# Attention of eight heads: divide the exponentials before they are transposed, with a new order of the whole pipeline

## The reference

```
hid = _group_norm(xr, norm_w, norm_b)
qkv = jnp.einsum('oc,bcl->bol', qkv_w, hid) + qkv_b[None, :, None]
qkv = qkv.reshape(b, H, 3, ch, L)
q, k, v = (qkv[:, :, 0], qkv[:, :, 1], qkv[:, :, 2])
weight = jnp.einsum('bhct,bhcs->bhts', q * scale, k * scale)
weight = jax.nn.softmax(weight.astype(jnp.float32), axis=-1)
a = jnp.einsum('bhts,bhcs->bhct', weight, v)
h = jnp.einsum('oc,bcl->bol', proj_w, a.reshape(b, c, L)) + proj_b[None, :, None]
return (x + h) / RESCALE
```

## Time and profile before

| | |
|---|---|
| median of 3 runs | 2169.7 us (2168.6 to 2170.22) |
| the profiled execution | 2170.37 us, of which span 2168.3 us |
| mean granted TensorE clock | 0.976 |
| busy: PE, DVE, ACT, POOL | 2076.3, 1820.4, 1527.8, 1278.3 us |
| share of the ending chain by engine | PE 91%, DVE 3%, POOL 2% |

### The profile page before, as it was taken

One profiled execution on the slowest core, in us unless ns is written; L12 is line 12 of the kernel. 1 busy time (PEld: TensorE's weight loads), 2 busy tenths in 40 slices (PEclk: granted clock), 3 DMA queues, 4 the chain that ended last, 5 costly groups with the idle time before them and its releaser, 6 DMA issues.

```text
span 2168.3 us, 58678 instructions
## 1 busy us (share of the span) xinstructions
PE 2076.3 (96%) x15232; PEld 1686.7 (78%) x15232; DVE 1820.4 (84%) x4359; ACT 1527.8 (70%) x5172; POOL 1278.3 (59%) x2954
## 2 busy tenths in 40 slices
PE   4679999999999999999999999999999999999987
PEld 3466888888888788888878888887888888788775
DVE  6778899988888998988899898888989888887532
ACT  2256777777777777777777777777777777777763
POOL 2455666666666666666666666666666666664311
PEclk8799999999999999999999999999999999999977
DMA  3000011001101100110110011011101100100000
GB/s 126 15 23 23 16 39 39 29 23 37 37 22 37 37 30 22 37 37 22 37 37 30 22 37 37 23 36 37 37 15 37 37 31 28 38 31 24 24 23 23
DMA packets 29828, 70.22 MB, mean 32 GB/s; under 512 B 6261, under 2 KB 7105, under 8 KB 29761
## 3 DMA queue, kind: packets, MB, share of 16 engines
q1 hardware_dynamic: 26928, 67.68, 9.0%
q10 hardware_dynamic: 2832, 1.73, 0.3%
HBM read 30.86 MB, written 12.85 MB: 20 GB/s over the span
## 4 chain that ended last, share of the span: by engine, by line
PE 91%; DVE 3%; POOL 2%; issue 2%; ACT 1%; SPq 1%; DMA 0%; POOLq 0%; DVEq 0%; ACTq 0%
PE ps_c L1166 19%; PE ps_a L1166 17%; PE ps_e L1166 17%; PE ps_b L1166 17%; PE ps_s L1166 10%; PE ps_s L1216 8%; POOL gn_t L579 1%; PE ps_a L1292 1%; DVE y L1158 1%; PE ps_e L1454 0%; PE ps_e L1292 0%; PE ps_b L1454 0%; PE ps_e L1399 0%; SPq L475 0%; ACT e L827 0%
## 5 line engine op out<-in xcount | busy, mean ns | idle before, releaser
L827 ACT ACTIVATE e<-ps_s,nm 98x196 f32<-98x196 f32 x1024 | 426.1, 446 | 89.9 <-DVE nm L956 89.8
L590 POOL TENSOR_SCALAR xn<-x,gn_scale,gn_shift 128x196 f32<-128x196 f32 x384 | 353.2, 933 | 20.8 <-POOL gn_shift L585 20.8
L1158 DVE SCALAR_TENSOR_TENSOR y<-opad,w_dw,y 128x406 f32<-128x406 f32 x512 | 301.8, 645 | 0.0
L1139 DVE SCALAR_TENSOR_TENSOR y<-xpad,w_dw,y 128x406 f32<-128x406 f32 x512 | 300.8, 640 | 0.0
L956 DVE TENSOR_REDUCE nm<-ps_s 98x4 f32<-98x784 f32 x256 | 240.6, 962 | 41.8 <-PE ps_s L1166 41.8
L834 ACT COPY pt<-ps_s 98x392 f32<-98x392 f32 x512 | 229.1, 503 | 42.6 <-PE ps_s L1216 41.8
L568 POOL TENSOR_TENSOR gn_t<-gn_group 128x4 f32<-128x4 f32 x96 | 34.3, 358 | 372.9 <-DVE gn_group L1006 286.5
L827 ACT ACTIVATION_READ_ACCUMULATOR e<-ps_s,nm 98x1 f32 x1024 | 231.6, 226 | 0.0
L1216 PE MATMUL ps_s<-w_eye,e 98*98 98x98 f32 x2048 | 204.6, 251 | 0.6 <-ACT e L827 0.6
L1216 PEld LDWEIGHTS ps_s<-w_eye,e 98*98 98x98 f32 x2048 | 186.3, 131 | 24.1 <-issue 16.2
L581 POOL TENSOR_SCALAR gn_t<-gn_t 128x4 f32<-128x4 f32 x288 | 119.7, 416 | 58.6 <-POOL gn_t L579 58.6
(11 more groups left out here) (245 smaller groups left out, 5596.8 us busy)
## 6 DMA issues: line engine op xcount, KB each, us to landing
x_in<-in_x SPq DMA_DIRECT2D x32, 392.0 KB, 3.1
x_res<-in_x SPq DMA_DIRECT2D x32, 392.0 KB, 3.3
x2b<-x SPq DMA_DIRECT2D x32, 392.0 KB, 2.6
out<-x SPq DMA_DIRECT2D x32, 392.0 KB, 2.6
out_pairs<-out SPq DMA_DIRECT2D x32, 392.0 KB, 3.5
w_q<-in_q SPq DMA_DIRECT2D x3, 256.0 KB
w_k<-in_k SPq DMA_DIRECT2D x3, 256.0 KB
w_v<-in_v SPq DMA_DIRECT2D x3, 256.0 KB
```

The lines of the kernel that those rows point to most:

```text
L590: g.tensor_scalar(dst[:, c, of_image(i)], src[:, c, of_image(i)], t.scale[:, j:j + 1], t.shift[:, j:j + 1], ALU.mult, ALU.add).then_inc(t. ...
L827: s.activation(e2[:, j, tc], tile(use)[0:HALF, of_image(tc)], ACT.Exp, bias=nm2[:, j, tc:tc + 1], accum_out=den2[:, 2 * i + tc, h:h + 1]). ...
L1139: v.scalar_tensor_tensor(out=dst, in0=window(xpad, c, k, CR), scalar=tap, in1=dst, op0=ALU.mult, op1=ALU.add).then_inc(conv1_steps.sem, 1)
L1158: v.scalar_tensor_tensor(out=dst, in0=window(opad, c, k, CR), scalar=tap, in1=dst, op0=ALU.mult, op1=ALU.add).then_inc(conv2_steps.sem, 1)
```

## The change

The exponentials of a head are divided by their sums in place, in `e2`, before PE transposes them. For this DVE takes reciprocals eight times a pair, for two heads each (`rden{g}_{m}`); heads 0 and 2 of each pass are then scaled by ACT (`less{g}_0`, `less{g}_2`), heads 1 and 3 by POOL (`less{g}_1`, `less{g}_3`), two instructions of 98x196 a head. The transposes wait for the scaled tiles. The steps `rden`, `rt`, `rep0`, `rep1`, their buffers and the weight `heads` go, and `proj` reads `a2`. All five tables have new numbers, and the shared PSUM banks a, b, c, e have new uses; the largest place is 819 instead of 760, so a pair now spans one table step more.

```diff
+                    for four in range(GROUPS):
+                        for j in range(1, HG, 2):
+                            p = pair_of(t, u, POOL_AT[f"less{four}_{j}"])
+                            if p is not None:
+                                h = HG * (four % 2) + j
+                                pool.wait_ge(rden_done.sem, rden_done.at(p, 2 * four + j // 2 + 1))
+                                for tc in range(2):
+                                    alone()
+                                    g.tensor_scalar(e2[:, j, tc], e2[:, j, tc], rden2[:, 2 * (four // 2) + tc, h:h + 1], None,
+                                                    ALU.mult).then_inc(p2_done[j].sem, 1)
...
-                    p = pair_of(t, u, ACT_AT["rt"])
-                    if p is not None:
-                        act.wait_ge(*full(p, "rt"))
-                        if has_before(p) and not comes_after("rt", latest("rep0", "rep1")):
-                            act.wait_ge(*full(p - 1, latest("rep0", "rep1")))
-                        s.copy(rt2[:, 0], tile("rt")[0:H2, 0:N2]).then_inc(rt_high.sem, 1)
...
+                            p = pair_of(t, u, ACT_AT[f"less{g}_{j}"]) if j % 2 == 0 else None
+                            if p is not None:
+                                h = HG * (g % 2) + j
+                                act.wait_ge(rden_done.sem, rden_done.at(p, 2 * g + j // 2 + 1))
+                                for tc in range(2):
+                                    s.activation(e2[:, j, tc], e2[:, j, tc], ACT.Copy,
+                                                 scale=rden2[:, 2 * i + tc, h:h + 1]).then_inc(p2_done[j].sem, 1)
...
+                            p = pair_of(t, u, DVE_AT[f"rden{g}_{m}"])
+                            if p is not None:
+                                for j in (2 * m, 2 * m + 1):
+                                    dve.wait_ge(*read(p, f"sc{g}_{j}"))
+                                h = HG * (g % 2) + 2 * m
+                                v.reciprocal(rden2[:, 2 * i:2 * i + 2, h:h + 2], den2[:, 2 * i:2 * i + 2, h:h + 2]
+                                             ).then_inc(rden_done.sem, 1)
...
-                                for source in elsewhere(use, f"sc{g}_{j}"):
-                                    pe.wait_ge(*read(p, source))
+                                pe.wait_ge(p2_done[j].sem, p2_done[j].at(p, 2 * g + 2))
...
-                            product(tile(use)[:, 0:N2], lambda k: heads[:, c], lambda k: rt2[:, k]).then_inc(filled(use), 1)
...
-                            product(tile(use)[:, 0:N2], lambda k: w["p2"][:, k, of_chunk(c)], lambda k: an2[:, :, k]
+                            product(tile(use)[:, 0:N2], lambda k: w["p2"][:, k, of_chunk(c)], lambda k: a2[:, :, k]
```

More of the change, by code:

```diff
@@ L104 @@
     "qb2": (128, KC), "kb2": (128, KC), "vb2": (128, KC), "p2": (128, KC, CH), "pb2": (128, KC),
-    "heads": (H2, KC, 128), "eye": (128, 128),
+    "eye": (128, 128),
     "gn3_w": (128, 4), "gn3_b": (128, 4), "q3": (128, KC, CH), "k3": (128, KC, CH), "v3": (128, KC, CH),
@@ L358, in build @@
         max2_done = Count("max2_done", UNITS // 2)
-        rden_done = Count("rden_done", 1)
-        rt_high = Count("rt_high", 1)
+        rden_done = Count("rden_done", 2 * GROUPS)
+        p2_done = [Count(f"p2_done{j}", 2 * GROUPS) for j in range(HG)]
         l3_less_steps = Count("l3_less_steps", 2 * 3)
@@ L660, in split_weights @@
                     s.copy(high, src).then_inc(early_high, 1)
-                s.copy(heads[:], w["heads"][:]).then_inc(early_steps, 1)
                 act.wait_ge(early_steps, EARLY_STEPS)
@@ L839, in step @@
                             if has_before(p):
-                                act.wait_ge(*read(p - 1, f"rep{g % 2}"))
+                                act.wait_ge(*full(p - 1, latest("proj0", "proj1")))
                             s.copy(a2[:, i, g % 2], tile(use)[:, 0:TOK]).then_inc(emptied(use), 1)
@@ L1051, in step @@
                                                    in1=xn1[:, c], op0=ALU.add, op1=ALU.add).then_inc(emptied(use), 1)
-                    p = pair_of(t, u, DVE_AT["rden"])
-                    if p is not None:
-                        for use in ends(*(f"sc{g}_{j}" for g in range(GROUPS) for j in range(HG))):
-                            dve.wait_ge(*read(p, use))
-                        if has_before(p):
-                            dve.wait_ge(*full(p - 1, "rt"))
-                        v.reciprocal(rden2[:], den2[:]).then_inc(rden_done.sem, 1)
-                    p = pair_of(t, u, DVE_AT["rt"])
-                    if p is not None:
-                        dve.wait_ge(rt_high.sem, rt_high.at(p, 1))
-                        v.tensor_tensor(rt2[:, 1], tile("rt")[0:H2, 0:N2], rt2[:, 0], ALU.subtract).then_inc(emptied("rt"), 1)
-                    for c in range(KC):
-                        use = f"rep{c}"
-                        p = pair_of(t, u, DVE_AT[use])
-                        if p is not None:
-                            dve.wait_ge(*full(p, use))
-                            if has_before(p) and not comes_after(use, latest("proj0", "proj1")):
-                                dve.wait_ge(*full(p - 1, latest("proj0", "proj1")))
-                            for source in ends(f"av{c}", f"av{2 + c}"):
-                                dve.wait_ge(*read(p, source))
-                            v.tensor_tensor(an2[:, :, c], tile(use)[:, 0:N2].rearrange("p (i n) -> p i n", i=2),
-                                            a2[:, :, c], ALU.mult).then_inc(emptied(use), 1)
+                    for g in range(GROUPS):
+                        i = g // 2
+                        for m in range(2):
+                            p = pair_of(t, u, DVE_AT[f"rden{g}_{m}"])
[5 more added lines that the diff above has]
+                                             ).then_inc(rden_done.sem, 1)
                     for c in range(KC):
@@ L1392, in step @@
                                ).then_inc(filled(use), 1)
-                    p = pair_of(t, u, PE_AT["rt"])
-                    if p is not None:
-                        pe.wait_ge(*free(p, "rt"))
-                        pe.wait_ge(rden_done.sem, rden_done.at(p, 1))
-                        for j in range(4):
-                            last = nc.tensor.transpose(tile("rt")[0:H2, j * HALF:(j + 1) * HALF], rden2[:, j],
-                                                       eye[0:HALF, 0:HALF])
-                        last.then_inc(filled("rt"), 1)
-                    for c in range(KC):
-                        use = f"rep{c}"
-                        p = pair_of(t, u, PE_AT[use])
-                        if p is not None:
-                            pe.wait_ge(*free(p, use))
-                            for source in elsewhere(use, "rt"):
-                                pe.wait_ge(*read(p, source))
-                            product(tile(use)[:, 0:N2], lambda k: heads[:, c], lambda k: rt2[:, k]).then_inc(filled(use), 1)
                     for c in range(KC):
@@ L1414, in step @@
                             pe.wait_ge(*free(p, use))
[L1415 removed]
+                            for source in elsewhere(use, *(f"av{g}" for g in range(GROUPS))):
                                 pe.wait_ge(*read(p, source))
[L1417 removed]
+                            product(tile(use)[:, 0:N2], lambda k: w["p2"][:, k, of_chunk(c)], lambda k: a2[:, :, k]
                                     ).then_inc(filled(use), 1)
```

19 lines of the change are left out of this document (7 added, 12 removed), and 73 rows, old and new, of tables (ACT_AT, BANK_USES, DVE_AT, PE_AT).

## The result

| | before | after |
|---|---|---|
| median | 2169.76 us (4 runs) | 2241.84 us (2240.12 to 2243.65, 4 runs) |
| ratio | | 1.0333 (95%: 1.032 to 1.0346) |
| span of the profiled execution | 2168.3 us | 2238.0 us |
| mean granted TensorE clock | 0.976 | 0.974 |

The change makes the kernel 3.3% slower. Forecast were 2178 us with a range to 2208, so the side was the more probable one, but the size is 72 us against 8.

A forecast was written before the change was run, and what follows sets the result against it. PE, never waiting, was taken as the bound with a period of 63.08 us. 63.08 - 1.17 + 1.3 + 0.1 = 63.31, and 31 x 0.23 = 7 us over the profiled execution gave 2178 us, range 2138 to 2208.

The forecast's parts named there:

- the side: Whole run: slower was given chance 0.46, faster 0.38, within 0.2% of no change 0.16.
- PE's period of before, PE as the bound: Loop before the change: PE never waits, its sequence is the 63.08 us period; no other engine becomes the bound by sum.
- gn1's chain, the hold by the taps, the queue behind it: Pass 0: DVE's taps hold POOL's xn, four done at 11.4 us; POOL's scalings and ACT's thirteen instructions follow late.
- 16 instructions ... 0.49 from start to start: POOL's added scalings, priced like xn at 0.49 us each, 7.9 us a pair; one operation less maybe cheaper.
- All else on PE stays, reordered: PE: only the reciprocals' transposes and spreading products leave, 1.17 us a pair, 36 us if nothing takes it back.
- Rival 3: Removed PE work leaves, but an unseen place takes about its size back or more, or another engine's order decides; chance 0.07.
- The stall, 1.3 + 0.1 us: PE waiting each pair: 1.3 us in pass 0 (bounds 0 to 3.4), 0.1 in passes 1 to 3 (0 to 0.4).
- Rival 1: POOL passes between DVE's taps, so pass 0 stalls only 0 to 0.8 us: 2146 us, range 2134 to 2160; chance 0.34.
- Rival 2: POOL is held in more passes, pass 2 too, costing 1.5 to 3 us a pair on top: 2239 us; chance 0.15.
- Filling and draining I cost at nothing: Start and end of the run: no added time, as DVE's first tap to last output is 762 places instead of 759.
- 31 periods are 1955 of 2170 us: Whole run before: 31 full periods, the rest filling and draining, so a change of the period counts 31 times.

The follow-up runs named there:

- experiment 3: Changed kernel, POOL scaling head 1 of each pass with two operations in place, head 3 with one operation into its own tensor: 2236.68 us.
- experiment 6: Changed kernel with both of POOL's heads scaled in place by two operations (times the reciprocal, plus 0.0): 2233.35 us, ratio 1.029.
- experiment 2: Kernel before, old order, with the division left out (no reciprocals, turning, spreading or multiplication): 2142.61 us, ratio 0.9871.
- experiment 1: Changed kernel, new order, with all 32 scalings of a pair left out, the eight reciprocals kept: 2194.63 us, ratio 1.0108.
- experiment 9: Kernel of experiment 6 with three steps moved: DVE's second reciprocals of pass 0 and ACT's head 2 scaling earlier, an L3 scaling later: 2227.51 us, ratio 1.0268.
- experiment 4: Changed kernel with heads 1 and 3 of pass 0 scaled by ACT as well, POOL keeping six heads: 2235.94 us, ratio 1.0302.
- experiment 8: Kernel of experiment 1 with two of PE's steps that waited for a shared bank put later: 2199.21 us, ratio 1.0138.

## Why the prediction was wrong

- **PE's period of before, PE as the bound; the side.** Right. With idle PE the period grew, and the excess stands where forecast first.
- **gn1's chain, the hold by the taps, the queue behind it.** The times are right to 0.3 us in three places (8.5, 10.5, 11.4), and so was the place of the stall: heads 1 and 3 of pass 0. The hold itself was mild: the four `xn1` take 2.90 us, of which the first starts beside the last of the eight taps, and none is held over a run of them. Of the lateness 0.9 us are the taps' by this (2.90 against four times 0.5), the rest is the chain's.
- **"16 instructions ... 0.49 from start to start", lower bound 0.4.** This term failed: 0.77 to 0.80. The rows offered xn, 128x196 with two operations, as the nearest, and I let the missing operation count as a saving. It costs 0.35 us (experiment 3). The bound should have been open upward, too. It made PE's wait for POOL 1.47 us a period instead of 0.2, but for the time that is 8 us (experiment 6): the price was wrong, and a right one would not have saved the forecast.
- **"All else on PE stays, reordered": 1.17 us a pair gained.** This is the step that failed most. It treats PE's sequence as a sum of durations that an order does not alter. The removed work is worth 0.78 in the old order (experiment 2), and the new order costs 1.20 of its own before a single scaling is in it (experiment 1). Pass 0 alone is 15.01 us long without scalings, not 14.3. Rival 3 named this case, "takes about its size back or more", and gave it 0.07.
- **The stall, 1.3 + 0.1 us.** The scalings cost 1.53 together, all in pass 0, inside the bounds given. That the size fits is luck in part: the argument had POOL's instruction at 0.49 us. With one of 0.43 (experiment 6) pass 0 loses 0.6 us and not 1.3, and pass 1 loses 0.5 more, which the argument did not foresee. The idle time was forecast as the price of one late engine; in truth three links stand within a microsecond of each other (POOL's scaling, ACT's queue, DVE's reading of proj0), so that taking POOL's away gives 8 us and ACT's 6 more (experiments 6, 9).
- **Rival 1** did not come: all of POOL's work in pass 0 was done as late as forecast, no earlier. **Rival 2** did not come either in its form: PE's waits for POOL are two a period, both in pass 0. That its 2239 us lie 3 from the measured time is chance.
- **"Filling and draining I cost at nothing."** The draining became 2.1 us shorter. The filling took 19.9 us more, the second term that was put at nothing and was not. The argument compared places of DVE's table from the first tap to the last output, and these say nothing of how long the engines wait in the filling. What holds them there I could not show.
- **"31 periods are 1955 of 2170 us."** Not so: there are 27 periods of 63.1 us, and the 31 intervals together are 1900.5. A change of the period counts 27 times in full, not 31.
- The sum, then, by experiments 1 and 2: the removed work gave 28 us instead of 36, the new order took 52 instead of nothing, the scalings 47 instead of 1.4 x 31 = 43. The forecast's 7 us and these 8 + 52 + 4 make 71, and 72 were measured. The last term comes close though it counts 31 periods: 1.53 x 27 is 41 of the 47 us, 2.4 stand in the filling (271.2 against 268.8), most of the rest in the draining.

## What to carry to other kernels

Split a change that comes with a new order before pricing it: run the old order without the removed work, and the new order without the added work. The difference between these two is the order's own price, which the sum of durations did not give here; it was 52 us, more than the 28 that the removed work gave. Then compare the two kernels stretch by stretch from start to start, since the waits with names were only 0.06 us a period apart. In this kernel, with four engines busy for 79 to 97% and every bank shared, removing 1.3 us of waits gave back 0.16 us a period (experiment 6), 1.5 us gave 0.17 (experiment 4), 0.5 us gave 0.25 (experiment 9), and 0.4 us gave nothing (experiment 8): ask for the next two links before counting a gain. And bound an instruction form that the trace does not show upward as well, even where it does less.

## What was unexpected of the hardware

GpSimd's multiplication of 98x196 fp32 by a per-partition factor took 0.77 to 0.78 us as one operation and 0.43 as two (with + 0.0), in one program, on the same data type (experiment 3). ScalarE's scaling of the same tile took 0.36 from start to start, as in L3. And a small instruction of gn1's chain on GpSimd, where the ten behind it in that chain take 0.20 to 0.51 us, started at 927.98 beside a maximum and was done at 929.89. GpSimd, then DVE, in the changed kernel:

```profile
927.98 1.91 POOL L580 TENSOR_TENSOR gn_t<-gn_y 128x4 f32<-128x4 f32 x1
```

```profile
926.65 1.20 DVE L1137 SCALAR_TENSOR_TENSOR y<-xpad,w_dw,y 128x406 f32<-128x406 f32 x2
927.77 0.96 DVE L966 TENSOR_REDUCE nm<-ps_s 98x4 f32<-98x784 f32 x1
928.66 1.18 DVE L1137 SCALAR_TENSOR_TENSOR y<-xpad,w_dw,y 128x406 f32<-128x406 f32 x2
```

The two taps began 0.7 us after it, and it ended with the second of them, at 929.84. The Trainium skill (SBUF — State Buffer, "SBUF: two separate sides") lets the one that starts first hold the port, and holds it for a single instruction; as with the 5.51 us of the earlier trace rows, the trace does not agree.
